# The front of a two-layer megakernel: normalising on GpSimd, and scaling weights between the tiles

## The reference, cut to what matters

```
x = x + L0_xattn(_layernorm(x), ctx, ...)        # 1024 sequential steps: two LSTM cells, attention over 64 rows
x = x + L0_ffn(_layernorm(x), ...)
x = x + L1_xattn(_layernorm(x), ctx, ...)
x = x + L1_ffn(_layernorm(x), ...)               # 8 experts

def _layernorm(x, axis=-1, eps=1e-05):
    m = jnp.mean(x, axis=axis, keepdims=True)
    v = jnp.var(x, axis=axis, keepdims=True)
    return (x - m) / jnp.sqrt(v + eps)
```

## Time and the profile before

| | |
|---|---|
| median of 3 runs | 8156.05 us (8155.39 to 8157.4) |
| the profiled execution | 8160.45 us, of which the span (first to last instruction) is 8158.7 us |
| `front` in it | 0 to about 55.2 us, where the first DMA of `scan` is issued |
| PE, DVE, ACT, POOL busy over the span | 88%, 54%, 41%, 4% |

### The profile page before, as it was taken

How to read it: one execution, slowest core, us unless ns; L and a number is a source line. 1 busy time by engine, 2 the same in 40 slices (tenths; PEclk the granted TensorE clock), 3 DMA queues, 4 the chain that set the end, 5 groups by cost and what they waited for, 6 DMA issues and landing times. The chain is left out here.

```text
span 8158.7 us, 998374 instructions
## 1 busy us (share of the span) xinstructions
PE 7204.2 (88%) x470544; PEld 6373.2 (78%) x470545; DVE 4419.2 (54%) x21132; ACT 3380.3 (41%) x17489; POOL 313.6 (4%) x332
## 2 busy tenths in 40 slices
PE   7888888888888888888888888888888888888869
PEld 6888888888888888888888888888888888856546
DVE  5555555555555555555555555555555555566822
ACT  3444444444444444444444444444444444452722
POOL 0000000000000000000000000000000000001632
PEclk8999999999999999999999999999999999989889
DMA  3000000000000000000000000000000000000143
GB/s 113 5 0 0 5 0 0 0 0 5 0 0 0 5 0 0 0 0 5 0 0 0 5 0 0 0 5 0 0 0 0 5 0 0 0 6 19 62 149 109
DMA packets 94638, 102.01 MB, mean 13 GB/s; under 512 B 46570, under 2 KB 81904, under 8 KB 93424
## 3 DMA queue, kind: packets, MB, share of 16 engines
q1 hardware_dynamic: 89200, 88.73, 3.5%
q0 software_dynamic: 5376, 12.63, 0.4%
HBM read 79.75 MB, written 23.67 MB: 13 GB/s over the span
## 5 line engine op out<-in xcount | busy, mean ns | idle before, releaser
L367 PE MATMUL scan_sums<-rec_wh,scan_hT 128*8 128x64 f32 (+1 forms) x163760 | 2521.0, 209 | 0.1
L367 PEld LDWEIGHTS scan_sums<-rec_wh,scan_hT 128*8 128x8 f32 x163760 | 2130.2, 89 | 0.4 <-issue 0.2
L499 DVE STREAM_TRANSPOSE scan_sums<-scan_sums 128x64 f32<-128x64 f32 (+1 forms) x6144 | 1461.4, 252 | 1226.6 <-PE scan_sums L367 1226.4
L367 PE MATMUL scan_sums<-rec_wa,scan_aT 128*8 128x64 f32 (+2 forms) x81920 | 1158.4, 209 | 425.8 <-ACT scan_aT L454 425.5
L367 PEld LDWEIGHTS scan_sums<-rec_wa,scan_aT 128*8 128x8 f32 (+1 forms) x81920 | 1025.3, 89 | 557.1 <-ACT scan_aT L454 556.5
L367 PE MATMUL scan_sums<-rec_wx,scan_xT 128*8 128x64 f32 (+2 forms) x81920 | 1369.0, 209 | 2.9 <-issue 2.0
L367 PE MATMUL scan_sums<-rec_wi,scan_hT 128*8 128x64 f32 (+2 forms) x81920 | 1157.4, 209 | 35.0 <-issue 6.5
L367 PEld LDWEIGHTS scan_sums<-rec_wi,scan_hT 128*8 128x8 f32 (+1 forms) x81920 | 1025.4, 89 | 166.7 <-DVE scan_hT L591 159.9
L367 PEld LDWEIGHTS scan_sums<-rec_wx,scan_xT 128*8 128x8 f32 (+1 forms) x81920 | 1107.4, 89 | 3.8 <-issue 2.7
L438 ACT ACTIVATE scan_tanh_ig<-scan_sums 128x16 f32<-128x16 f32 x2048 | 378.0, 185 | 1620.2 <-DVE scan_sums L499 1618.8
L433 ACT ACTIVATE scan_sums<-rec_bias 128x192 f32<-128x192 f32 x2050 | 686.7, 335 | 296.0 <-PE scan_sums L415 6.1
(11 more groups left out here) (266 smaller groups left out, 6592.6 us busy)
## 6 DMA issues: line engine op xcount, KB each, us to landing
experts_bias<-in_b SPq DMA_DIRECT2D x40, 640.0 KB, 4.5
moe_w<-in_w SPq DMA_DIRECT2D x16, 1024.0 KB, 15.3
slots_x<-scan_blank SPq DMA_DIRECT2D x40, 129.0 KB
experts_x<-slots_x SPq DMA_DIRECT2D x40, 129.0 KB, 2.0
w_xres<-in_x_steps SPq DMA_DIRECT2D x8, 512.0 KB, 11.0
w_xres<-in_x SPq DMA_DIRECT2D x4, 1024.0 KB, 12.2
x_rows<-w_xres SPq DMA_DIRECT2D x4, 1024.0 KB, 8.6
a_rows<-scan_stage SPq DMA_DIRECT2D x224, 16.0 KB, 1.5
```

The lines of the kernel that those rows point to most:

```text
L367: last = nc.tensor.matmul(sums[layer][BANK[g]][32 * j:32 * j + rows, 0:width], state[:, k, first:first + rows], weight[:, k, j, 64 * g + 3 ...
L499: nc.vector.transpose(turned[l][g][:, 0:width], sums[l][g][:, 0:width]).then_inc(gates_turned[l][g], 1)
```

## The change

POOL takes over the subtract and multiply of each tile (`tensor_scalar` with two operands of one column each). DVE keeps the moments and the reciprocal. The moments have four copies (`AHEAD`) in place of two, and DVE waits for `xn_done` before it overwrites one. The one semaphore `scan_in` becomes one for each weight. ACT's nine scalings move into its loop, behind the copies of tiles 20 to 22, 24 to 26 and 28 to 30 (iterations 21 to 23, 25 to 27, 29 to 31); DVE's weight work moves into iterations 9, 10, 13, 17, 21 and 29. The order of the DMAs stays as it is.

```diff
-def norm_memory(pool):
+def norm_memory(pool, copies=2):
...
-    m = {n: [pool.sbuf(f"norm_{n}{i}", [P, w]) for i in range(2)] for n, w in
+    m = {n: [pool.sbuf(f"norm_{n}{i}", [P, w]) for i in range(copies)] for n, w in
...
+        AHEAD = 4
+        norm = norm_memory(m, AHEAD)
-        fold_in, scan_in, bias_in = m.sem("fold_in"), m.sem("scan_in"), m.sem("bias_in")
+        fold_in, bias_in = m.sem("fold_in"), m.sem("bias_in")
+        scan_in = {name: m.sem(f"{name}_in") for name in ("wx", "wa", "wh0", "wi1", "wh1", "woh")}
...
-                    sp.dma_start(w[name][:], ins[name]).then_inc(scan_in, 16)
+                    sp.dma_start(w[name][:], ins[name]).then_inc(scan_in[name], 16)
...
                 pool.wait_ge(zeroed, 6)
+                for n in range(NT):
+                    pool.wait_ge(norm["rstd_done"], n + 1)
+                    if n >= 2:
+                        pool.wait_ge(turned_done, n - 1)
+                    nc.gpsimd.tensor_scalar(xn[n % 2][:], tile_at(n), norm["mean_var"][n % AHEAD][:, 0:1], norm["rstd"][n % AHEAD][:],
+                                            ALU.subtract, ALU.mult).then_inc(xn_done, 1)
...
             def _(act):
                 act.wait_ge(norm["eps_done"], 1)
+                def scale(name, part):
+                    act.wait_ge(scan_in[name], 16)
+                    gates = w[name][:].rearrange("p k j (g u) -> p (k j) g u", g=GATES)
+                    of, by = ((slice(0, 2), 0.25), (slice(2, 3), 0.5), (slice(3, 4), 0.25))[part]
+                    nc.scalar.activation(gates[:, :, of, :], gates[:, :, of, :], ACT.Copy, scale=by).then_inc(halved, 1)
+                scaled_at = {4 * g + 1 + part: (name, part) for g, name in ((5, "wh0"), (6, "wi1"), (7, "wh1")) for part in range(3)}
                 for n in range(NT + 1):
                     if n < NT:
-                        norm_scalar(nc, act, norm, n + 1, n % 2)
+                        norm_scalar(nc, act, norm, n + 1, n % AHEAD)
                     if n > 0:
                         act.wait_ge(turned_done, n)
                         nc.scalar.activation(xT_all[:, :, P * (n - 1):P * n],
                                              turned[(n - 1) % 2][:, 0:D].rearrange("p (c n) -> p c n", c=KC), ACT.Copy).then_inc(xT_done, 1)
-                act.wait_ge(scan_in, 6 * 16)
-                for name in ("wh0", "wi1", "wh1"):
...
+                    if n in scaled_at:
+                        scale(*scaled_at[n])
...
             def _(dve):
+                between = {9: sum_biases, 10: place_biases, 13: keep_folded, 17: lambda: halve("wx"), 21: lambda: halve("wa"), 29: halve_woh}
                 for n in range(NT + 1):
                     if n < NT:
                         if n % B == 0:
                             dve.wait_ge(x_in[n // B], 16)
-                        norm_moments(nc, dve, norm, n + 1, n % 2, tile_at(n))
+                        if n >= AHEAD:
+                            dve.wait_ge(xn_done, n + 1 - AHEAD)
+                        norm_moments(nc, dve, norm, n + 1, n % AHEAD, tile_at(n))
                     if n > 0:
-                        if n > 2:
-                            dve.wait_ge(turned_done, n - 2)
-                        norm_apply(nc, dve, norm, n, (n - 1) % 2, tile_at(n - 1), xn[(n - 1) % 2][:]).then_inc(xn_done, 1)
+                        s = (n - 1) % AHEAD
+                        dve.wait_ge(norm["std_done"], n)
+                        nc.vector.reciprocal(norm["rstd"][s][:], norm["std"][s][:]).then_inc(norm["rstd_done"], 1)
+                    if n in between:
+                        between[n]()
```

More of the change, by code:

```diff
@@ L135, in front @@
         m = Pool(nc, ctx, "front")
-        norm = norm_memory(m)
+        AHEAD = 4
+        norm = norm_memory(m, AHEAD)
         xn = [m.sbuf(f"xn{i}", [P, D]) for i in range(2)]
@@ L226, in _, with sum_biases, place_biases, keep_folded @@
                 nc.vector.memset(norm["eps"][:], EPS).then_inc(norm["eps_done"], 1)
+                def sum_biases():
+                    dve.wait_ge(bias_in, 16 * 5)
+                    nc.vector.tensor_tensor(bias[0][:], bias[0][:], bias[1][:], ALU.add).then_inc(scaled, 1)
+                def place_biases():
+                    dve.wait_ge(scaled, 1)
+                    for at, gates in ((0, slice(0, 1)), (2, slice(3, 4))):
+                        nc.vector.tensor_scalar(w["bias"][:, :, at:at + 1, :], bias[0][:, :, gates, :], 0.5, None, ALU.mult).then_inc(scaled, 1)
+                    nc.vector.scalar_tensor_tensor(w["bias"][:, :, 1, :], bias[0][:, :, 1, :], 0.5, bias[0][:, :, 2, :],
+                                                   ALU.mult, ALU.add).then_inc(scaled, 1)
+                def keep_folded():
+                    dve.wait_ge(folded, 1)
+                    for k in range(2):
+                        nc.vector.tensor_scalar(w["kp"][:, k, :, :].rearrange("p b s -> p (b s)"), kp[k][:, 0:B * S], 0.5,
+                                                None, ALU.mult).then_inc(scaled, 1)
+                        nc.vector.tensor_tensor(w["vp"][:, k, :, :].rearrange("p j u -> p (j u)"), vp[k][:, 0:D], bo[:],
+                                                ALU.add).then_inc(scaled, 1)
+                def halve(name):
+                    dve.wait_ge(scan_in[name], 16)
+                    halve_sigmoid_gates(nc, w[name][:].rearrange("p k j (g u) -> p (k j) g u", g=GATES), 1.0, scaled)
+                def halve_woh():
+                    dve.wait_ge(scan_in["woh"], 16)
+                    nc.vector.tensor_scalar(w["woh"][:], w["woh"][:], 0.5, None, ALU.mult).then_inc(scaled, 1)
+                between = {9: sum_biases, 10: place_biases, 13: keep_folded, 17: lambda: halve("wx"), 21: lambda: halve("wa"), 29: halve_woh}
                 for n in range(NT + 1):
```

## The result

The changed kernel takes 8168.82 us (median of 19 runs, 8164.88 to 8173.03) against 8156.42 us (19 runs) for the kernel before: a ratio of 1.0015, interval 1.0008 to 1.0021. So it is slower by 12.4 us. The range leaves out one slow run of 8861.6 us, whose granted clock was 0.725 where the others have 0.98. The prediction was 8157.0, range 8151 to 8163: the sign of its sum was right, the size was not, and the time lies outside the range.

A forecast was written before the change was run, and what follows sets the result against it. The prediction took DVE to bound the front's loop before, and the closed ring over ACT after. A 5.94 us tail removed against 6.9 us added made the front 0.9 us longer: 8156.05 to 8157.0 us, range 8151 to 8163.

The forecast's parts named there:

- What bounds the kernel, and the size at stake: Stage before the scan: 54.73 of 8158.7 us, its loop bound by DVE; a 0.2% difference would be 16.3 us.
- The ring: Front's tile loop: root n+1 behind copy n-1 on ACT closes a two-tile circle, 2.04 us a turn, 2.34 after.
- The price of the apply on POOL: POOL's subtract and multiply of one tile: 0.60 us, plus 0.11 us later start, against 0.41 on DVE.
- The part up to 25.62 at zero: Front through the fold: DVE's waits, 2.13 us for x and 4.79 under the fold, cover any slower pace; cost zero.
- Eight turns: Tile 14 to tile 30: one turn at 2.09 and seven at 2.34 us, 18.47 against 17.18, so +1.3 us.
- Scalings in the ring, and contention: Front's loop: ACT's scalings between copy and root add 3.86 us; DVE's halvings delaying POOL add 1.35, bounds 0 to 2.6.
- The last tile: Front's end: from tile 30's reciprocal to the end of copy 31, 2.86 us, ending at 55.65.
- The sum: Whole front: the 5.94 us tail goes, 6.9 us come into the loop and its last tile; 0.9 us longer, 47%.
- Four copies help nothing: DVE's moments in the front: further copies gain nothing, since DVE waits for the root behind ACT's copy.
- POOL is slow: POOL's apply takes 0.94 us and contention is 2.6: +5.2 us, 8161.3; chance 17%.
- POOL is quick: POOL's apply takes 0.39 us without contention: -2.3 us, 8153.7; chance 25%.
- It does what it says: Front's scalings hide in ACT's idle time and the pace falls to DVE's 0.7 us: -11.9 us, 8144; chance 3%.

The follow-up runs named there:

- roots ahead: The changed kernel with ACT's copies one place further behind its square roots; 8163.97 us, ratio 1.0004 to the kernel before.
- POOL alone: The changed kernel with the weights' work of ACT and DVE behind the tile loop again; 8168.68 us, ratio 1.0015 to the kernel before.
- every second tile on POOL: The changed kernel with POOL applying only odd tiles, DVE the others, and ACT's copies one place further behind its roots; 8160.17 us, ratio 0.9998.
- two copies: The changed kernel with AHEAD = 2, so two copies of the moments instead of four; 8186.70 us, ratio 1.0032 to the kernel before.
- prices on POOL: The kernel before with a chain of single POOL instructions on scratch columns during the front; 8155.49 us, one run.

## Why the prediction was wrong, by its own steps

- **What bounds the kernel, and the size at stake**: right. The front was some 55 us of 8158.7, and a microsecond of it is one of the time.
- **The ring**: right. It closes as read, and it is opened by one place in ACT's order (roots ahead). A turn at 1.22 us for the apply comes out by my terms as 2.04 - 0.41 + 1.22 + 0.11 = 2.96; measured 2.86.
- **The price of the apply on POOL**: this step failed. I put 0.60 us, between 0.39 and 0.73 to 0.94; measured 1.23 alone, 1.22 in the kernel beside nothing else, and 1.275 as the mean of 32. The bracket came from an affine select below and a tensor_tensor above, and the apply lies outside it. The Trainium skill's rule that I had weighed (GPSIMD Engine Reference, 8. Key points, about twice as fast on VectorE) gives an estimate of 0.82 and points the right way; measured it is three times, 1.22 against 0.41.
- **The part up to 25.62 at zero**: this step failed too, and not by the price alone. I took DVE's wait for x at tile 8 as cover for everything in front of the fold. The wait did cover DVE, whose moments of tile 8 are 0.2 us later than before; but the fold stands behind tile 8's square root and apply, and they hang on the ring, on POOL's price and on the biases of iteration 9. Even at 0.60 us the apply would have been 0.30 us longer there without cover by my own terms (0.60 - 0.41 + 0.11). The fold started 2.14 us later, took 0.65 less in this trace, and tile 14's reciprocal is 1.98 us later than before where I had +0.25.
- **Eight turns**: +1.3 forecast; 8 x 2.86 less 17.18 is +5.70. The first turn (30.84 to 33.70) took 2.86 like the others, not 0.25 us less as I had it: its transposes already took 0.69 us.
- **Scalings in the ring, and contention**: +3.86 and +1.35 forecast. The eight turns together took 58.98 - 30.84 = 28.14 us, so 5.26 over 8 x 2.86, against 5.21. Single turns show them: 44.52 - 40.10 = 4.42 (0.94 and 0.62 more than 2.86) and 47.90 - 44.52 = 3.38 (0.52 more). Both sums were right to the tenth. The scalings were right one by one; that the three waits came out at 1.39 us is partly luck, 0.68, 0.62 and 0.09 where I had 0.55, 0.5 and 0.3. How POOL and DVE exclude each other is not settled by it. The Trainium skill's lock (SBUF — State Buffer, Who interferes with whom), by which one waits out the whole of the other's instruction, agrees in that POOL is late by about the length of the first halving (0.68 and 0.74 us), and my upper end, both instructions, is excluded. But that first halving had only 0.50 and 0.56 us left when POOL's apply was due, and DVE's second halving (L120, at 40.77 and 34.45) took its usual 0.42 and 0.41 us while POOL's apply was still going on, which speaks against a lock in that direction.
- **The last tile**: 2.75 us from tile 30's reciprocal to the end of copy 31 before; 2.86 forecast, 3.85 measured (62.83 - 58.98). I had let ACT's last scaling set this end. At 1.22 us it is POOL: tile 31's apply stands behind tile 30's (59.25 for 2.42 us), and ACT idles 0.30 us before the last copy.
- **The sum**: 1.98 + 5.70 + 5.26 + 1.10 - 5.94 = +8.1 us in the front, where I had +0.9. Of the 7.2 us between them 4.4 stand in the turns, 1.7 up to tile 14 and 1.0 in the last tile, and nearly all of it hangs on the one price, 0.62 us above mine.
- **Four copies help nothing**: wrong. They are worth 13.7 us here; I had looked only at the wait that ends last with them.
- **The rivals**: *POOL is slow* was the nearest, and its price was still too low by 0.28 us a tile. *POOL is quick* stands as a mechanism: with a copy of 0.40 us the front ends at 51.06. *It does what it says* is out: in the order as written the scalings hid neither at 1.22 us nor with the copy of 0.40, where the turn from tile 24 to 26 still took 42.71 - 39.76 = 2.95 us against 2.00 without a scaling. *Slower by more than 0.2%* did not come, at 1.0015, though the mechanism named for it did: POOL's apply lengthened every turn, at half the price that it wanted. *Loading of code* did not occur: the first two applies, 2.46 us, are like the others.
- **The separate semaphores, and the first scan steps**: right. From the start of the scan to the first `make_a` it is 24.9 us before and 25.0 after.

What stays open: the front explains 8.1 of the 12.4 us between the medians, or 8.6 (2.14 of the fold's start and 6.45 behind the fold) if the fold's own length is left out as chance. 8.1 lies inside the interval (1.0008 to 1.0021 is 6.5 to 17 us). The profiled executions differ by 8.2 us in span, but the one of the kernel before, 8160.45 us, is slower than each of its 19 runs (the highest is 8157.4), and the one of the changed kernel, 8168.65, is at its median; so this pair of traces can't show the other 4 us. POOL alone shows them too (9.0 us of front, 12.5 of median). From the start of the scan to the end of the span the traces vary between 8095.2 (every second tile on POOL) and 8108.1 us (two copies); both belong to session 2, in which the kernel before itself spread from 8150.0 to 8167.9 us, and in sessions 1 and 3 they lie between 8099.1 and 8103.4. No experiment told this part apart, and its cause is not known.

## What to carry to other kernels

Before work is moved to an engine that looks idle, price that exact form of instruction there: the same shape in another operation is no bound. Then look for the ring in which the work stands, since in a closed ring an idle engine's latency counts in full. Where a wait is to cover a slower step, follow what hangs on the step: the wait covers only the engine that waits. Where two copies of a buffer become four, ask what the third would wait for, and where an order has a root behind a copy, try it one place further ahead before anything is moved.

## What the runs showed of the hardware

- On POOL a tensor_scalar with two operations and constants took 0.21 us for one column and 3.3 ns more for each further one; with two one-column operands it took 1.23 us for 128x256. One operation with a constant took 0.86, a copy of the same size 0.40, and a tensor_tensor 0.61 (run prices on POOL).
- DVE's fp32 apply of the same size takes 0.41 us, so POOL is three times as slow for it.
- A POOL tensor_scalar that is due while DVE halves 1024 columns was 0.62 to 0.68 us late, about that instruction's length (0.68 and 0.74 us). The other way round, in the run with every second tile on POOL, such a halving that started 0.99 us behind POOL's apply took 0.88 us where it took 0.69 in the kernel before.
